# Grouped attention in steps of two batches: one unrolled pipeline over half of the tokens at a time in place of four looped rounds

## The chip, the cores and the metric

The kernel runs on one core of a Trainium2 chip. The metric is the device time of one execution in microseconds, the median of repeated runs. The engines are TensorE (PE; PEld is its weight load), VectorE (DVE), ScalarE (ACT), GpSimd (POOL) and SyncE (SP, which issues the loads).

## The reference

Two layers over 1024 tokens (four batches of 256) of width 256, each an attention and a feed-forward part with a layer norm of the sum behind it. What matters here is the attention inside the last part, with 16 query heads, 4 key and value heads of width 128, rotary embedding and a causal softmax:

```python
H, KV, HD = (16, 4, 128)
def attention(x, wq, wk, wv, wo):
    q = (x @ wq).reshape(b, s, H, HD)
    k = (x @ wk).reshape(b, s, KV, HD)
    v = (x @ wv).reshape(b, s, KV, HD)
    q, k = apply_rope(q, cos, sin), apply_rope(k, cos, sin)
    k, v = jnp.repeat(k, rep, axis=2), jnp.repeat(v, rep, axis=2)
    scores = jnp.einsum('bqhd,bkhd->bhqk', q, k) / np.sqrt(HD)
    scores = jnp.where(causal[None, None], scores, jnp.finfo(scores.dtype).min)
    out = jnp.einsum('bhqk,bkhd->bqhd', jax.nn.softmax(scores, axis=-1), v)
    return out.reshape(b, s, H * HD) @ wo
h = hidden_states + attention(rmsnorm(hidden_states, norm1_w), wq, wk, wv, wo)
```

## The kernel before

The kernel is a chain of blocks, one for each part; in a block every engine has its own program, and the programs meet through semaphores. `layer1_grouped_attention` is the block of this change. It follows a norm that leaves the turned activations as a high and a low part (`c.xTh`, `c.xTl`), and it is followed by the routed experts.

Products of weights and activations are made of three matmuls per 128 rows of contraction (`split_product`: high by low, low by high, high by high), so a projection of 512 tokens to one head is six matmuls of 512 columns. Scores, transposes and values are plain float32.

**Tiling.** A round is one key head with its four query heads, over all 1024 tokens. It has 16 items, an item being one query head in one batch: 256 queries against 256 keys. The causal half is used: 128 queries see 128 keys and the other 128 see 256, so an item has 384 columns of scores. The four rounds are turns of a loop that all engines run (`Fori(0, HKV)`).

**Order.** TensorE's program in a round goes over t from 0 to 19: scores of item t (a mask matmul and two more), at t = 1, 2, 5, 6, 9, 10, 13, 14 half a query projection of the next head (`project_at`), at t = 16 and 17 the two halves of the next round's keys, the output products of item t-4, the three transposes of item t-2, the values of item t-3. Scores and projections take turns on two PSUM banks, 4 and 5, in an order given by `ring`; `freed` makes each wait for whoever last read its bank. Bank 6 has the turned probabilities, bank 7 the values' result, and banks 0 to 3 sum the output projection over all heads of all rounds. Inside a round the items overlap; a round's items are all finished before the next one's scores begin. The last round too projects keys and queries for a round to come.

**The other engines.** VectorE takes the negative maxima of the scores (L1501, L1502), rotates projections (L1478 to L1480: by cosine, then by sine in two halves), takes reciprocals, copies most of the turned probabilities to SBUF (L1518), and makes the low part of an item's result (L1523). It also splits all weights into high and low: the pieces of the next round (L1533, L1535) and each head of wo (L1485, L1487), and copies the round's values out of `v_all` (L1510). ScalarE has the exponentials with their sums (L1555), the high part of the result (L1566), the other turned copies (L1561). GpSimd adds the two products of a rotation (L1452) and multiplies the probabilities by the reciprocals (L1461, L1462). SyncE loads the next round's weights and wo once the last ones are split.

Of the kernel before, what the change touches and what calls it, by code (L numbers as in the profile page):

```python
# [1362 lines left out]
def layer1_grouped_attention(c, pre, spent):  # L1363

    nc, ps = c.nc, c.ps
    PIECES = 1 + GROUP
    with ExitStack() as ctx:  # L1367
        def sb(name, shape, dt=F32):
            return c.tile(ctx, "e_" + name, shape, dt)

        stage, wh, wl, rope = pre.stage, pre.wh, pre.wl, pre.rope
        wo = sb("wo", [P, GROUP, D])
        wo_hi = sb("wo_hi", [P, GROUP, D], F32R)
        wo_lo = sb("wo_lo", [P, GROUP, D], F32R)
        v_all = sb("v_all", [P, NT, HKV * P])
        k_T = spent.stage[:, 0:TOK]
        v = sb("v", [P, NT, P])
        q_T = sb("q_T", [P, 2, TOK])
        by_cos = sb("by_cos", [P, 2, 512])
        by_sin = sb("by_sin", [P, 2, 512])  # L1380
        neg_max = sb("neg_max", [P, 4, 2])
        sums = sb("sums", [P, 4, 2])
        rsum = sb("rsum", [P, 4, 2])
        probs = sb("probs", [P, 4, CAUSAL])
        probsT = sb("probsT", [P, 2, CAUSAL])
        o_hi = sb("o_hi", [P, 2, SEQ], F32R)
        o_lo = sb("o_lo", [P, 2, SEQ], F32R)
        table = sb("table", [P, 1])

        stage_in, wo_in = c.sems(ctx, "e", "stage_in wo_in")  # L1390
        pe_sems = proj_ps, v_ps, s_ps, t_ps, pv_ps, wo_ps = c.sems(ctx, "e", "proj_ps v_ps s_ps t_ps pv_ps wo_ps")
        dve_sems = w_hi, w_split, turned_ps, nm_ready, rs_ready, v_copied, pT_ready, wo_high, wo_split, o_low = c.sems(
            ctx, "e", "w_hi w_split turned_ps nm_ready rs_ready v_copied pT_ready wo_high wo_split o_low")
        act_sems = v_ready, p_ready, o_high = c.sems(ctx, "e", "v_ready p_ready o_high")
        pool_sems = roped, pn_ready = c.sems(ctx, "e", "roped pn_ready")
        block = ctx.enter_context(nc.Block())
        ITEMS = GROUP * BATCH

        ring = []
        for t in range(ITEMS):
            ring.append(("s", t))
            if t % 4 in (1, 2):
                ring.append(("q", 2 * (t // 4 + 1) + t % 4 - 1))
        ring += [("k", 0), ("k", 1)]
        at = {key: n for n, key in enumerate(ring)}
        order = [r for r in ring if r[0] != "s"]
        first = [("k", 1), ("k", 0), ("q", 2 * GROUP), ("q", 2 * GROUP + 1)]  # L1410
        project_at = {t: ("q", 2 * (t // 4 + 1) + t % 4 - 1) for t in range(ITEMS) if t % 4 in (1, 2)}
        project_at |= {ITEMS: ("k", 0), ITEMS + 1: ("k", 1)}

        split_at = {3: 0, 4: 1, 7: 2, 8: 3, 11: 4}

        split_out_at = {5: 3, 9: 0, 12: 1, ITEMS: 2}

        def projected(g, key):
            return LEAD + len(first) + len(order) * g + order.index(key) + 1

        def freed(eng, g, key):

            n = at[key] - 2
            last, g = ring[n % len(ring)], g - 1 if n < 0 else g
            if last[0] == "s":
                eng.wait_ge(p_ready, LEAD + 2 * (ITEMS * g + last[1] + 1))
            else:
                eng.wait_ge(turned_ps, projected(g, last))

        def half_of(key):  # L1430
            return slice(key[1] % 2 * 512, (key[1] % 2 + 1) * 512)
# [12 lines left out]

        @block.gpsimd
        def _(pool):
            give_lead(pool, pool_sems)

            def rotate(key, count, slot):
                pool.wait_ge(turned_ps, count)  # L1450
# [118 lines left out]
        def _(pe):  # L1569
# [17 lines left out]
            for t in range(2):  # L1587
                project_v(t)
# [601 lines left out]
```

## Time and profile before

| | |
|---|---|
| time before, median of 3 runs | 1087.45 us (1087.24 to 1087.92) |
| the profiled execution | 1085.36 us, its span 1083.6 us |
| busy in the span | PE 968.6 (89%), DVE 722.8 (67%), ACT 479.5 (44%), POOL 380.8 (35%) |
| granted TensorE clock, mean over the span | 0.963 |
| the stage from 592.9 to 868.1 us | PE busy 247.4, DVE 211.6, ACT 106.7, POOL 120.0 |

The span is the time from the first instruction to the last; the execution's own time has something around it. Busy shares of an engine are a mean over blocks with different limits, so the stage's own numbers count here. Matmuls overlap in the array, so that TensorE's busy time says less than the distance from one start to the next.

### The profile page before, as it was taken

The page shows a single profiled execution, that of the slowest core. Times are in us where ns is not written, and L with a number is a line of the kernel's source. Part 1 is how long each engine was busy: PE and PEld are TensorE (multiplying, and loading weights), DVE is VectorE, ACT ScalarE, POOL GpSimd, SP SyncE. Part 2 cuts the span into 40 slices and gives each one's busy share as a digit, 9 for nine tenths or more (in the row PEclk, how much of TensorE's full clock was granted, in tenths as well). Part 3 has the DMA queues.
Part 4 walks back from the last instruction along what each step waited for, and adds up shares of the span by engine and source line. Part 5 has one row for each costly group of instructions (what it writes and reads, how often), then busy time and mean ns, then how long its engine had stood idle before and what let it go on. Part 6 is the DMA issues. An engine that isn't in the chain of part 4 may idle for free. (4 is left out here: it accounts for less than half of the span.)

```text
span 1083.6 us, 19692 instructions
## 1 busy us (share of the span) xinstructions
PE 968.6 (89%) x7078; PEld 790.2 (73%) x7087; DVE 722.8 (67%) x1353; ACT 479.5 (44%) x1082; POOL 380.8 (35%) x416
## 2 busy tenths in 40 slices
PE   9788989978999999999997899897989879899970
PEld 5455666647888888788884688786868738899970
DVE  3476767875555555665555687787868767688845
ACT  4221345534445446545444344343434353566630
POOL 2000300005676676576650344453444405000005
PEclk9899989999999999999999999999999979999995
DMA  4000100023324333334321000000104016755503
GB/s 173 1 2 2 30 2 2 2 83 112 109 84 121 110 92 112 105 87 122 108 60 44 5 21 25 19 24 0 44 0 165 0 59 246 279 205 204 205 30 116
DMA packets 55435, 86.87 MB, mean 80 GB/s; under 512 B 4800, under 2 KB 45504, under 8 KB 53184
## 3 DMA queue, kind: packets, MB, share of 16 engines
q1 hardware_dynamic: 53824, 81.66, 23.2%
q0 software_dynamic: 1536, 4.20, 1.2%
q8 instruction: 49, 0.80, 0.3%
q14 instruction: 26, 0.21, 0.1%
HBM read 74.83 MB, written 11.01 MB: 79 GB/s over the span
## 5 line engine op out<-in xcount | busy, mean ns | idle before, releaser
L1555 ACT ACTIVATE e_probs<-ps,e_neg_max 128x128 f32<-128x128 f32 (+1 forms) x128 | 52.8, 417 | 112.7 <-DVE e_neg_max L1502 112.7
L1109 DVE TENSOR_TENSOR d_s_m<-ps,d_decay 128x768 f32<-128x768 f32 x64 | 58.3, 952 | 50.6 <-PE ps L1272 50.6
L123 PE MATMUL ps<-xTl,d_wh 128*128 128x512 f32 x192 | 80.1, 417 | 0.0
L123 PE MATMUL ps<-xTh,d_wh 128*128 128x512 f32 x192 | 76.4, 398 | 0.0
L123 PE MATMUL ps<-xTh,d_wl 128*128 128x512 f32 x192 | 76.3, 397 | 0.0
L123 PE MATMUL ps<-wl_gated,f_wh 128*128 128x256 f32 x240 | 69.1, 288 | 5.8 <-issue 3.7
L1192 ACT ACTIVATE d_gated_hi<-d_gated 128x512 fp32r<-128x512 f32 x32 | 20.2, 632 | 110.6 <-DVE d_gated L1115 110.6
L123 PE MATMUL ps<-wh_gated,f_wl 128*128 128x256 f32 x240 | 68.1, 284 | 0.0
L123 PE MATMUL ps<-wh_gated,f_wh 128*128 128x256 f32 x240 | 68.0, 283 | 0.0
L1452 POOL TENSOR_TENSOR e_q_T<-e_by_cos,e_by_sin 128x512 f32<-128x512 f32 x34 | 43.7, 1287 | 49.4 <-DVE e_by_sin L1480 49.4
L787 ACT ACTIVATE g_probs<-ps,g_neg_max 128x256 f32<-128x256 f32 (+1 forms) x128 | 43.3, 423 | 37.7 <-DVE g_neg_max L730 37.7
L1098 DVE TENSOR_TENSOR wl_gated<-d_q_T,wh_gated 128x512 fp32r<-128x512 f32 x32 | 23.7, 741 | 53.7 <-ACT wh_gated L1171 53.7
L958 POOL TENSOR_TENSOR d_wh<-d_stage,d_nought 128x512 fp32r<-128x512 f32 x32 | 44.3, 1383 | 42.2 <-PE ps L123 29.1
L1821 DVE TENSOR_TENSOR f_wl<-f_stage,f_wh 128x1024 fp32r<-128x1024 f32 x45 | 54.8, 1221 | 5.7 <-ACT f_wh L1947 4.7
L1795 POOL DMA_INDIRECT xT<-slot_outs,f_slots x8 | 7.9, 987 | 143.2 <-DMA slot_outs<-f_rows 141.1
L132 PE MATMUL ps<-warm 128*128 128x512 bf16 x170 | 47.6, 437 | 9.8 <-PEq L1367 3.2
L1461 POOL TENSOR_TENSOR e_probs<-e_probs,e_rsum 128x128 f32<-128x128 f32 x64 | 27.7, 432 | 78.8 <-DVE e_rsum L1507 78.8
L123 PEld LDWEIGHTS ps<-wl_gated,f_wh 128*128 128x128 f32 x240 | 45.6, 190 | 6.4 <-issue 6.3
L123 PE MATMUL ps<-xTl,e_wh 128*128 128x512 f32 x88 | 39.5, 449 | 11.9 <-DVE e_by_sin L1480 5.8
L1947 ACT ACTIVATE f_wh<-f_stage 128x1024 fp32r<-128x1024 f32 x45 | 47.2, 1051 | 6.5 <-DMA f_stage<-in_w_experts 5.1
L966 POOL TENSOR_TENSOR d_wh<-d_stage,d_nought 128x256 fp32r<-128x256 f32 x32 | 26.9, 840 | 63.7 <-PE ps L123 63.7
L123 PEld LDWEIGHTS ps<-xTl,d_wh 128*128 128x128 f32 x192 | 36.5, 190 | 12.8 <-issue 5.5
(364 smaller groups left out, 3203.4 us busy)
## 6 DMA issues: line engine op xcount, KB each, us to landing
f_stage<-in_w_experts SPq DMA_DIRECT2D x15, 1536.0 KB, 6.8
d_decay<-in_decay SPq DMA_DIRECT2D x32, 384.0 KB, 3.8
d_stage<-in_w_decay SPq DMA_DIRECT2D x32, 256.0 KB, 3.4
d_stage<-in_w_decay SPq DMA_DIRECT2D x32, 128.5 KB, 3.5
d_stage_v<-in_w_decay SPq DMA_DIRECT2D x32, 128.0 KB, 2.3
d_stage<-in_w_decay SPq DMA_DIRECT2D x32, 128.0 KB, 2.6
slot_rows<-warm SPq DMA_DIRECT2D x1, 3840.0 KB, 13.6
slot_outs<-f_rows SPq DMA_DIRECT2D x15, 256.0 KB, 2.1
```

Source lines behind the costliest of these rows:

```text
L123: mm = pe.matmul(out, w(k), x(k), start=(n == 0), stop=(n == 3 * len(ks) - 1))
L132: pe.matmul(out, c.warm16[:, 0:P], c.warm16[:, 0:out.shape[1]], start=True, stop=True)
L787: ex = act.activation(probs[:, n % KEPT, i, cols], ps[:, banks(n) + i, cols], ACT.Exp, bias=neg_max[:, n % 4, t, i:i + 1])
L958: pool.tensor_tensor(wh, qk, self.nought[:].unsqueeze(1).broadcast_to((P, KD, 2 * P)), ALU.add).then_inc(self.qk_high, 1)
L966: pool.tensor_tensor(wh, g, self.nought[:].unsqueeze(1).broadcast_to((P, KD, P)), ALU.add).then_inc(self.g_high, 1)
L1098: dve.tensor_tensor(q_lo, q_T[:], q_hi.bitcast(F32), ALU.subtract).then_inc(qk_lo, 1)
L1109: dve.tensor_tensor(s_m[:, s % 2, 2 * b:2 * b + 2, :], ps[:, 2 + 2 * b:4 + 2 * b, 0:CAUSAL], decay[:], ALU.mult).then_inc(sm_ready, 1)
L1452: pool.tensor_tensor(dst, by_cos[:, slot, :], by_sin[:, slot, :], ALU.add).then_inc(roped, 1)
L1461: pool.tensor_tensor(probs[:, u % 4, 0:P], probs[:, u % 4, 0:P], rsum[:, u % 4, 0:1].broadcast_to((P, P)), ALU.mult).then_inc(pn_ready, 1)
L1555: act.activation(probs[:, t % 4, cols], bank[:, cols], ACT.Exp, bias=neg_max[:, t % 4, b:b + 1], accum_out=sums[:, t % 4, b:b + 1]).then_i ...
L1821: dve.tensor_tensor(wl[j % 2][:, cols], stage[j % 2][:, cols], wh[j % 2][:, cols].bitcast(F32), ALU.subtract).then_inc(w_split, 1)
L1947: act.activation(wh[j % 2][:, PARTS[part]], stage[j % 2][:, PARTS[part]], ACT.Copy).then_inc(w_high, 1)
```

## The change

The attention runs unrolled in 32 steps. A step is one query head in two batches: steps 0 to 15 are the 16 heads over the first 512 tokens, steps 16 to 31 the same over the others. Both batches' scores lie in banks 2 and 3, their turned probabilities in 4 and 5, their values' result in 6, every projection in 7, and the output sums of one half in banks 0 and 1, which are read out (`add`) and cleared after the half. VectorE's maxima, copies and reciprocals, ScalarE's and VectorE's parts of the result and GpSimd's multiplications take both batches in one instruction.

In a step TensorE turns the probabilities of step s-2 ahead of the scores of step s, then projects (the queries of step s+2, or first the next keys where s % 4 is 2), then takes the values of step s-2 and the output products of step s-3; in steps with s % 4 = 2 the queries are projected last. Four of the eight value products move from the prologue to the end of steps 8, 9, 11 and 12.

All split weights are kept (`wh_more`, `wl_more`, `wo_hi`, `wo_lo` for all heads), so that the second half splits none. The high parts are now copied by ScalarE, one query head of wo and up to two pieces per step; the low parts of the projections are made by VectorE ahead of the maxima, those of wo by GpSimd. wo comes in 16 loads of one head, four heads ahead. `v_all` is read directly. `by_cos`, `by_sin`, `k_T`, `o_hi`, `o_lo` and `wo` lie in buffers of parts that are done. In `build`, the decay attention's weights are held only until that part is done.

The core of the diff, with eight columns of indentation left out and blank lines omitted:

```diff
+    HALF = TOK // 2
+    STEPS = 2 * HQ
+    PROJ, VALUES_OF = 7, 6
+    KEPT, KEPT_T = 3, 2
...
+def turns_at(s):
+    turns = [("k", (s + 2) // 4)] if s % 4 == 2 and s + 2 < STEPS else []
+    return turns + ([("q", s + 2)] if s + 2 < STEPS else [])
+first = [("k", 0), ("q", 0), ("q", 1)]
+order = first + [key for s in range(STEPS) for key in turns_at(s)]
+nth = {key: n for n, key in enumerate(order)}
+values_at = {8: 4, 9: 5, 11: 6, 12: 7}
+def pieces_at(s):
+    g, j = s // 4 + 1, s % 4
+    return [(g, piece) for piece in ((0, 1), (2, 3), (4,), ())[j]] if g < HKV else []
+pieces = [key for s in range(STEPS) for key in pieces_at(s)]
...
+    for s in range(HQ):
+        if s % 4 == 3 and s // 4 + 2 < HKV:
+            sp.wait_ge(w_split, (1 + GROUP) * (s // 4 + 1))
+            sp.dma_start(stage[:], c.dram["w_grouped"][s // 4 + 2]).then_inc(stage_in, 16)
+        if s + 4 < HQ:
+            sp.wait_ge(wo_split, s + 1)
+            load_out(s + 4)
...
+    def normalised(s):
+        pool.wait_ge(rs_ready, s + 1)
+        for t, cols in enumerate((slice(0, P), slice(P, CAUSAL))):
+            part = probs[:, s % KEPT, :, cols]
+            mul = pool.tensor_tensor(part, part, rsum[:, s % 4, t, :].unsqueeze(2).broadcast_to((P, 2, cols.stop - cols.start)), ALU.mult)
+        mul.then_inc(pn_ready, 1)
+    for key in first:
+        rotate(key)
+    for s in range(STEPS):
+        turns = turns_at(s)
+        for key in turns[:1]:
+            rotate(key)
+        normalised(s)
+        for key in turns[1:]:
+            rotate(key)
+        if s < HQ:
+            pool.wait_ge(wo_high, s + 1)
+            pool.tensor_tensor(wo_lo[:, s, :], wo[:, s % 4, :], wo_hi[:, s, :].bitcast(F32), ALU.subtract).then_inc(wo_split, 1)
...
+    def copy_turned(s):
+        dve.wait_ge(t_ps, s + 1)
+        need(dve, pv_ps, s - KEPT_T + 1)
+        dve.tensor_copy(probsT[:, s % KEPT_T], ps[:, 4:6, 0:CAUSAL]).then_inc(pT_ready, 1)
+    def maxima(s):
+        dve.wait_ge(s_ps, s + 1)
+        need(dve, p_ready, s - 3)
+        pair = ps[:, 2:4, :]
+        dve.tensor_reduce(neg_max[:, s % 4, 0], pair[:, :, 0:P], X, ALU.max, negate=True)
+        dve.tensor_reduce(neg_max[:, s % 4, 1], pair[:, :, P:CAUSAL], X, ALU.max, negate=True).then_inc(nm_ready, 1)
+    def reciprocals(s):
+        dve.wait_ge(p_ready, s + 1)
+        need(dve, pn_ready, s - 3)
+        dve.reciprocal(rsum[:, s % 4], sums[:, s % 4]).then_inc(rs_ready, 1)
+    def low_out(s):
+        dve.wait_ge(o_high, s + 1)
+        dve.tensor_tensor(o_lo[:, s % 2, :], ps[:, VALUES_OF, :], o_hi[:, s % 2, :].bitcast(F32), ALU.subtract).then_inc(o_low, 1)
+    def low_weights(key):
+        g, piece = key
+        dve.wait_ge(w_high, pieces.index(key) + 1)
+        dve.tensor_tensor(wl_more[:, g - 1, piece], stage[:, piece], wh_more[:, g - 1, piece].bitcast(F32), ALU.subtract).then_inc(w_split, 1)
+    def add(half):
+        dve.wait_ge(wo_ps, HQ * (half + 1))
+        for bank in range(2):
+            two = slice(4 * half + 2 * bank, 4 * half + 2 * bank + 2)
+            dve.tensor_tensor(c.y[:, two, :], ps[:, bank, :].rearrange("p (t d) -> p t d", t=2), c.x[:, two, :], ALU.add).then_inc(y_ready, 1)
...
+    for key, bank in zip(first, (PROJ, VALUES_OF, PROJ)):
+        rotate(key, ps[:, bank, :])
+    for s in range(STEPS + 3):
+        if 2 <= s < STEPS + 2:
+            copy_turned(s - 2)
+        if 1 <= s <= STEPS:
+            for key in pieces_at(s - 1):
+                low_weights(key)
+        if s == HQ + 3:
+            add(0)
+        turns = turns_at(s)
+        if s < STEPS:
+            maxima(s)
+        for key in turns[:1]:
+            rotate(key, ps[:, PROJ, :])
+        if s < STEPS:
+            reciprocals(s)
+        if 2 <= s < STEPS + 2:
+            low_out(s - 2)
+        for key in turns[1:]:
+            rotate(key, ps[:, PROJ, :])
+    add(1)
...
+    def exps(s):
+        act.wait_ge(nm_ready, s + 1)
+        need(act, t_ps, s - KEPT + 1)
+        need(act, rs_ready, s - 3)
+        for t, cols in enumerate((slice(0, P), slice(P, CAUSAL))):
+            for i in range(2):
+                ex = act.activation(probs[:, s % KEPT, i, cols], ps[:, 2 + i, cols], ACT.Exp, bias=neg_max[:, s % 4, t, i:i + 1],
+                                    accum_out=sums[:, s % 4, t, i:i + 1])
+        ex.then_inc(p_ready, 1)
...
+    for s in range(STEPS + 2):
+        if s < STEPS:
+            exps(s)
+        if s >= 2:
+            high_out(s - 2)
+        for key in pieces_at(s) if s < STEPS else ():
+            high_weights(key)
+        if s < HQ:
+            high_out_weights(s)
+        if s in values_at:
+            copy_values(values_at[s])
...
-    with pe.Fori(0, HKV) as g:
-        for t in range(ITEMS + 4):
-            if t < ITEMS:
-                b = t % 4
-                if b == 0:
-                    pe.wait_ge(roped, LEAD + len(first) + len(order) * g + 2 * (t // 4))
-                freed(pe, g, ("s", t))
...
+    def free_bank(bank):
+        if bank == PROJ and held:
+            sem, count = held[-1]
+            pe.wait_ge(sem, count)
...
+        g, piece = piece_of(key)
+        if g and key in order[3:]:
+            pe.wait_ge(w_split, pieces.index((g, piece)) + 1)
+        free_bank(bank)
...
+    def scores(s):
+        if s == 0:
+            pe.wait_ge(v_ready, 4)
+        need(pe, p_ready, s)
+        pe.wait_ge(roped, max(nth["q", s], nth["k", s // 4]) + 1)
+        q, keys = q_T[:, s % 2, :], k_T[:, s // 4 % 2, :]
+        for i in range(2):
+            pe.matmul(ps[:, 2 + i, 0:CAUSAL], c.ident16[:], c.neg16[:], start=True, stop=False)
+        for i in range(2):
+            bank, at = ps[:, 2 + i, :], i * SEQ
+            pe.matmul(bank[:, 0:P], q[:, at:at + P], keys[:, at:at + P], start=False, stop=False)
+            mm = pe.matmul(bank[:, P:CAUSAL], q[:, at + P:at + SEQ], keys[:, at:at + SEQ], start=False, stop=True)
+        mm.then_inc(s_ps, 1)
+    def turn(s):
+        pe.wait_ge(pn_ready, s + 1)
+        need(pe, pT_ready, s)
+        if s == 0:
+            pe.wait_ge(v_ready, 4)
+        for i in range(2):
+            for n in range(3):
+                mm = pe.transpose(ps[:, 4 + i, n * P:(n + 1) * P], probs[:, s % KEPT, i, n * P:(n + 1) * P], c.ident)
+        mm.then_inc(t_ps, 1)
...
+        if s == HQ:
+            pe.wait_ge(y_ready, 2)
+            clear()
...
+    for s in range(STEPS + 3):
+        if 2 <= s < STEPS + 2:
+            turn(s - 2)
+        if s < STEPS:
+            scores(s)
+        turns = turns_at(s)
+        for key in turns[:1]:
+            project(key)
+        if 2 <= s < STEPS + 2:
+            values(s - 2)
+        if s >= 3:
+            project_out(s - 3)
+        for key in turns[1:]:
+            project(key)
+        if s in values_at:
+            project_values(values_at[s])
```

## Rows read from the trace of the kernel before

**Rows 1.** The page's first line.
```profile
span 1083.6 us, 19692 instructions
```

**Rows 2.** Windows: prologue and first round; us, engine busy (instructions), PE clock, DMA share, GB/s.
```profile
592.90:613.20 20.30, 19.25 (x75) 14.90 (x76) 11.22 (x18) 5.07 (x9) 5.32 (x4) 0.92 0.16 58
613.20:676.30 63.10, 57.04 (x348) 48.71 (x348) 49.47 (x120) 26.28 (x92) 28.68 (x42) 1.00 0.06 20
```

**Rows 3.** Timeline of TensorE inside round one: start us, us, engine, line, op, form.
```profile
651.52 0.49 PE L1634 MATMUL ps<-consts,e_probs 128*128 128x128 f32 x3
...
654.04 0.49 PE L1634 MATMUL ps<-consts,e_probs 128*128 128x128 f32 x3
654.37 0.60 PE L1643 MATMUL ps<-e_probsT,e_v 128*128 128x256 f32 x2
...
655.02 0.33 PE L1609 MATMUL ps<-neg,ident 128*128 128x384 bf16 x1
...
657.24 0.28 PE L1626 MATMUL ps<-e_wo_lo,e_o_hi 128*128 128x256 f32 x1
...
657.95 0.49 PE L1634 MATMUL ps<-consts,e_probs 128*128 128x128 f32 x3
```

**Rows 4.** Timeline of TensorE: first, sixteenth and next round's first scores.
```profile
613.25 0.33 PE L1609 MATMUL ps<-neg,ident 128*128 128x384 bf16 x1 [0.98 <-ACT e_v_all L1546]
...
662.93 0.33 PE L1609 MATMUL ps<-neg,ident 128*128 128x384 bf16 x1
...
676.39 0.33 PE L1609 MATMUL ps<-neg,ident 128*128 128x384 bf16 x1
```

**Rows 5.** Waits, 613.2 to 868.2: who for whom, us in total, times, longest.
```profile
PEld ps L123 <- DVE e_by_sin L1480: 9.9, 16, 1.8
PEld ps L1609 <- POOL e_q_T L1452: 6.7, 4, 1.7
```

**Rows 6.** Groups by form, 592.9 to 868.2: busy us, mean ns of one, idle before.
```profile
L1452 POOL TENSOR_TENSOR e_q_T<-e_by_cos,e_by_sin 128x512 f32<-128x512 f32 x34 | 43.7, 1287 | 49.4 <-DVE e_by_sin L1480 49.4
L1462 POOL TENSOR_TENSOR e_probs<-e_probs,e_rsum 128x256 f32<-128x256 f32 x64 | 39.2, 613 | 0.0
...
L123 PE MATMUL ps<-xTh,e_wl 128*128 128x512 f32 x88 | 35.4, 402 | 0.0
...
L1478 DVE TENSOR_TENSOR e_by_cos<-ps,e_rope 128x512 f32<-128x512 f32 x44 | 30.0, 681 | 21.6 <-PE ps L123 21.6
...
L1566 ACT ACTIVATE e_o_hi<-ps 128x256 fp32r<-128x256 f32 x64 | 24.6, 385 | 15.4 <-PE ps L1644 14.5
```

**Rows 7.** Timeline of VectorE in the gated attention, where instructions are paired.
```profile
216.32 0.43 DVE L729 TENSOR_REDUCE g_neg_max<-ps 128x2 f32<-128x256 f32 x1 [0.48 <-PE ps L852]
...
217.26 0.95 DVE L735 COPY g_probsT<-ps 128x768 f32<-128x768 f32 x1
```

**Rows 8.** Timeline of ScalarE in round four: an item's exponentials and what follows.
```profile
853.98 0.37 ACT L1555 ACTIVATE e_probs<-ps,e_neg_max 128x128 f32<-128x128 f32 x1 [1.19 <-DVE e_neg_max L1502]
...
854.91 0.39 ACT L1566 ACTIVATE e_o_hi<-ps 128x256 fp32r<-128x256 f32 x1
```

**Rows 9.** Timeline, gated attention: six transposes and the copy that waits for them.
```profile
225.77 0.85 PE L843 MATMUL ps<-consts,g_probs 128*128 128x128 f32 x6 [0.35 <-DVE g_probsT L735]
...
226.66 0.96 DVE L735 COPY g_probsT<-ps 128x768 f32<-128x768 f32 x1 [1.03 <-PE ps L843]
```

**Rows 10.** Timeline: a matmul of the prologue, the additions at the end.
```profile
594.76 0.63 PE L123 MATMUL ps<-xTl,e_wh 128*128 128x512 f32 x1
...
865.56 2.48 DVE L1538 TENSOR_TENSOR y<-ps,x 128x512 f32<-128x512 f32 x4 [0.61 <-PE ps L1626]
```

**Rows 11.** Tile e_wo: splits on VectorE; ns min/median/max, first and last start.
```profile
L1485 DVE CAST e_wo_hi<-e_wo x19: 279/1147/1179, 608.9 to 858.8; 128x256 fp32r<-128x256 f32 x19
L1487 DVE TENSOR_TENSOR e_wo_lo<-e_wo,e_wo_hi x19: 424/425/1402, 609.3 to 860.0; 128x256 fp32r<-128x256 f32 x19
```

**Rows 12.** DMA issues: one grouped weight load, KB, median us to landing.
```profile
e_stage<-in_w_grouped SPq DMA_DIRECT2D x5, 640.0 KB, 4.0
```

More of the change, by code:

```diff
@@ L1407, in layer1_grouped_attention @@
[L1407 to L1431, printed above, removed]
+        stage, rope = pre.stage, pre.rope
+        wh_more = sb("wh_more", [P, HKV - 1, 1 + GROUP, KD, P], F32R)
@@ L1482, in _ @@
-            dve.wait_ge(pre.tables_in, 16)
-            def split_out(head, n):
-                dve.tensor_copy(wo_hi[:, head], wo[:, head]).then_inc(wo_high, 1)
-                dve.wait_ge(wo_high, LEAD + n)
-                dve.tensor_tensor(wo_lo[:, head], wo[:, head], wo_hi[:, head].bitcast(F32), ALU.subtract).then_inc(wo_split, 1)
-            for n, key in enumerate(first):
-                rotate(key, LEAD + n + 1, n % 2, ps[:, 4 + at[key] % 2, :])
-            dve.wait_ge(wo_in, 16)
-            for head in range(GROUP - 1):
-                split_out(head, head + 1)
@@ L1586, in _ @@
-            project(first[1])
-            for t in range(2):
-                project_v(t)
-            for bank in range(4):
-                pe.matmul(ps[:, bank, :], c.warm16[:, 0:P], c.warm16[:], start=True, stop=False, skip_group_check=True)
-            pe.wait_ge(turned_ps, LEAD + 2)
-            project(first[2])
-            for t in range(2, 4):
-                project_v(t)
-            pe.wait_ge(turned_ps, LEAD + 3)
-            project(first[3])
-            for t in range(4, NT):
-                project_v(t)
@@ new lines, in project_values, with clear @@
+                if bank == PROJ:
+                    held.append((v_ready, t + 1))
+            def clear():
+                for bank in range(2):
+                    pe.matmul(ps[:, bank, :], c.warm16[:, 0:P], c.warm16[:], start=True, stop=False, skip_group_check=True)
+            def scores(s):
[11 more added lines that the diff above has]
+                mm.then_inc(s_ps, 1)
@@ new lines, in project_out @@
+            def project_out(s):
+                head = s % HQ
+                if s < HQ:
+                    pe.wait_ge(wo_split, head + 1)
+                if s == HQ:
+                    pe.wait_ge(y_ready, 2)
+                    clear()
+                for o, ws, ready in ((o_hi, (wo_lo, wo_hi), o_high), (o_lo, (wo_hi,), o_low)):
+                    pe.wait_ge(ready, s + 1)
+                    for t in range(4):
+                        for w in ws:
+                            mm = pe.matmul(ps[:, t // 2, t % 2 * D:(t % 2 + 1) * D], o[:, s % 2, t * P:(t + 1) * P], w[:, head, :],
+                                           start=False, stop=False, skip_group_check=True)
+                mm.then_inc(wo_ps, 1)
```

285 lines of the change are left out of this document (99 added, 186 removed).

## The prediction

> **What bounds the kernel now.** I read the page first: the span is 1083.6 us [rows 1]. Then I cut the trace into stretches. The grouped attention runs from 592.9 to 868.2, one prologue of 20.3 us and four identical rounds of 63.1 us, TensorE busy in 57 of the 63.1 and at clock 1.00, VectorE busy in 49.5, the others under 29 [rows 2]. Nothing outside this stage is changed, so the sum is made inside it.
>
> TensorE's timeline inside a round gives the price of its work. Two items without a projection start 2.52 us apart (651.52 to 654.04), one with a projection takes 3.91 (654.04 to 657.95), so a projection costs 1.39 us and an item 2.52: transposes 0.33, values 0.65, scores some 0.83, output products 0.71 [rows 3]. The work of the whole stage is thus 64 items, 161.3 us, plus projections. There are 4 before the loop and 10 in each of four rounds, and 8 value products of the same six matmuls: 52 x 1.39 = 72.3. The four clearing matmuls are under 1, I take 0.8. Together 234.4 us out of 275.4 (592.9 to 868.3). TensorE stands still, or waits, for 41.0 us.
>
> Where these 41 us lie is seen from the first instruction of each item (L1609). The first scores of round one stand at 613.25 and the sixteenth at 662.93, the next round begins at 676.39 [rows 4]. From the sixteenth scores to the next round the work is 4 transposes less one already done, 4 value and 5 output products and 2 projections, about 0.8 + 1.0 + 2.6 + 3.5 + 2.8 = 10.7, but it takes 13.46. The first four items of a round lack most of their older work, yet the round as a whole is 63.1 against 16 x 2.52 + 13.9 = 54.2. So a round loses 8.9 us, four lose 35.6, mostly because each fills and drains the pipeline of items. The waits agree: TensorE's loads wait for the rotation on VectorE 9.9 us and the scores for the rotated queries on GpSimd 6.7 [rows 5], both at such places. TensorE's order of work is the bound, with bubbles at the loop's ends.
>
> **The change, part by part.** *Fewer projections.* The loop's last round projects keys and queries for a fifth group that doesn't exist, 4 x 1.39 = 5.6 us. The new order has 8 key and 32 query projections: 40, and 8 value products. Work: 161.3 + 48 x 1.39 + 0.8 = 228.8.
>
> *One pipeline of 32 steps instead of four of 16 items.* Per step TensorE does turn(s-2), scores(s), a projection, values(s-2), out(s-3): 1.39 + 2 x 2.52 = 6.43 us. Whether the others keep up I work out with prices of paired instructions. VectorE: a rotation is 3 instructions of about 0.69 at 0.70 spacing, 2.12; low_out of 512 columns is priced as one of them, the same kind of instruction of the same width from the same memories [rows 6]. The gated attention has the pair forms already: both maxima issue in 0.94 us and end within 1.02, the 768-wide copy takes 0.95 [rows 7]. With a reciprocal of 0.15 a plain step asks 0.95 + 1.02 + 2.12 + 0.17 + 0.72 = 5.0 us of VectorE. ScalarE: the four exponentials with read-outs of one item end 0.93 after they begin (853.98 to 854.91) [rows 8], so 1.86 a step, plus high_out at no more than twice today's 0.385 for half its width, 0.77, and up to three weight copies of 0.385: under 3.8. GpSimd: 1.29 for a rotation, 0.61 and 1.29 for the two normalisations [rows 6], and 0.65 for wo_lo: 3.9. A step with a key projection (s = 2, 6, ..., 26) adds 2.12 to VectorE and 1.39 to TensorE. So TensorE is the longest in each.
>
> Being longest is not enough where engines wait in order, so I followed a plain step from the moment turn(s-2) begins. From TensorE's slot to VectorE's start I count 0.24, from six transposes of 0.65 at 225.77 to the copy at 226.66 [rows 9]; back and to ScalarE 0.1. TensorE: turn to 0.65, scores to 2.3, projection to 3.7, values to 5.0, out to 6.4. VectorE: copy 0.9 to 1.85, maxima 2.5 to 3.55, rotation 3.9 to 6.0, reciprocal 6.2, low_out 6.3 to 7.0. ScalarE: exponentials 3.6 to 5.5, high_out to 6.2. Then each wait of TensorE is met ahead of time: values want the copy (1.85 against 3.7), the next scores the exponentials, since banks 2 and 3 are now single (5.5 against 7.1), the next projection its bank (6.0 against 8.7), the next out low_out (7.0 against 11.4), turn(s) the normalised probabilities (about 8.1 against 12.9). The move of the transposes ahead of the scores costs nothing: their data are a whole step old, and the scores behind them have 1.6 us of room. What is late next is the rotation after a key step: two rotations run to 2.4 into the next step, where TensorE wants the bank at 2.3, a wait of about 0.2, 7 times (the first of them counted with the start, below).
>
> *The waits that stay*, followed the same way. Slow clock at the head as now: some seven matmuls of 0.63 instead of 0.40 [rows 6, 10], at 0.2 each 1.4 us. Before the first scores 0.6 (they wait for value copy 4, whose bank they use). Steps 0 to 3 lack old work and run on the chain scores, maxima, exponentials and normalisation: 23.5 us for 18.9 of work, 4.6. Key steps 1.3. Step 11, where a key's late rotation meets a value product in the same bank, 0.5. Step 19, where add(0) of 1.4 us stands ahead of the maxima, 0.8. Steps 30 on, 23.6 us for 18.1 of work, with the last two additions (now four, 2.48 us [rows 10]) in it, 5.5, and 0.3 to the next block. Sum 15.0. Stage: 228.8 + 15.0 = 243.8, or 31.6 less than 275.4.
>
> *Weights split once.* The high halves move to ScalarE, where some 2.5 us of each step are free; the output weights' low halves move to GpSimd. VectorE keeps 15 subtractions in 9 steps (s = 1, 2, 3 mod 4, up to 11), ahead of the maxima. Alone one takes 0.424. But this very form has once taken 1.402, and the cast ahead of it, 0.279 at best, has a median of 1.147 [rows 11]: GpSimd was at work beside it. So a collision is worth 0.87 to 0.98. GpSimd normalises just then (0.9 to 2.8 of a step), so I expect most of the 15 to meet it. Bounds: none exposed, 0 (a gain is excluded, the subtractions are done today as well); all 15 at 0.98 exposed, 14.7. The scores' 1.6 us of room takes most of it; I put in 2.0. The Trainium skill, "SBUF — State Buffer", in the part on the memory's doors, says of this pair of engines that the one that starts first holds the shared port for its whole instruction; the spread of 279 to 1179 ns for one form agrees with that, and by its rule every one of the 15 would wait out the rest of a 0.6 or 1.3 us instruction, which is the upper bound's case.
>
> *Loads.* SyncE issues 16 smaller loads of wo in place of 5, each four steps ahead of use, and three of the stage, each issued a step before ScalarE wants it; 640 KB land in 4.0 us [rows 12], a step is 6.4. The later ones are issued only after w_split, so step 4's copy comes nearest, with 2 us of room, and ScalarE is not the bound there. The copy of v (four of them) and the table loads in the loop go; they lie on VectorE and ScalarE and I cost them at nothing. Below nothing they can't go: TensorE's stream is counted whole.
>
> **The sum.** -31.6 + 2.0 = -29.6 us. The profiled execution took 1085.4 us for its span of 1083.6; the median of the runs is 1087.45, 2.1 more than it. The difference is carried over: a span of about 1054 and a median of 1087.45 - 29.6 = 1057.9, about 1058.
>
> **The rivals.**
> *A, forecast*: TensorE's order sets the pace, small waits. 1053 to 1063.
> *B, fewer waits*: the first steps fill faster than I think and no split is exposed. The 15.0 falls to 10, nothing for collisions: 1087.45 - 36.6 = 1051. For it: the middle of today's rounds goes at 2.52 and 3.91 without a stop [rows 3]. Against it: the fill hangs on the chain of one item, which is priced from rows.
> *C, VectorE binds in the splitting steps*: three rounds with 5 subtractions each, VectorE 4 x 5.0 + 2.12 + 5 x 1.41 = 29.2 us against TensorE's 27.1 in a round, and all collisions exposed: 1056 + 14.7 = 1071, half exposed 1064. For it [rows 11]; against it, GpSimd is idle half the time.
> *D, the other side, TensorE's clock*. In the prologue now, after TensorE stood still ahead of this block, matmuls ran at 0.63 instead of 0.40 and the stretch shows 0.92 granted, that is partly the lower level, 1.2 of 2.4 GHz [rows 2, 6, 10]. If the new order's short stops (bank 7 freed late, single score banks) let the clock fall again and again, work done at the lower level costs its time once more. It decides from 29.6 us of full-speed work on, an eighth of the 228.8; at a sixth, 38 us, the result is 1096. Against it: the loop of today has longer stops at each round's end and shows 1.00. The Trainium skill, "TensorE: Matmul & The Clock Gate", under the second failure mode, warns that going round PSUM banks with small stops makes the clock swing; today's rounds don't bear it out.
> That the change doesn't do what it says isn't a case here: the four wasted projections and three of the drains are gone by the order of instructions alone.
>
> **How the numbers follow.** Chances: A 0.60, B 0.13, C 0.23, D 0.04. The time is A's, 1058. The range takes B to its 1051 and 2 more for a bound of my fill, and C up to its 1071: 1049 to 1071, leaving out D and the ends of B and C. A measurement of this kernel tells about 0.2%, 2.2 us, from no change. Faster holds A, B, C: 0.96; within 0.2% 0.01; slower 0.03.
>
> **What would show it.** In the changed kernel: about 244 to 246 us from the first projection to the last addition; steps 6.4 us apart by their first mask matmul, 7.8 to 8.0 where a key or value product joins; clock 1.00 after the prologue; TensorE's longest waits only in steps 0 to 3 and from 30 on; the maxima pair at 1.02, the copy at 0.95. The subtraction of wl_more with a mean over 1.0 us would speak for C; steps 4 to 11 well above 6.5 too. I am wrong if plain steps late in the stage (20 to 29) are above 6.8 us: then a loop through VectorE that I held to be met binds, or the clock does.

## The result, and the profile after

The changed kernel takes 1050.58 us in the median of 4 runs (1049.55 to 1051.54), against 1087.35 for four runs of the kernel before: a ratio of 0.9666, 95% interval 0.9648 to 0.9683, so 36.8 us less. The forecast was 1058, in a range of 1049 to 1071: the direction and the range hold, and the time is 7.4 us better than forecast, which is rival B's 1051.

The profiled execution took 1049.55 us. The page of the changed kernel, its first line and busy times, against [rows 1]:

```profile
span 1047.7 us, 18378 instructions
...
PE 948.7 (91%) x7053; PEld 785.2 (75%) x7063; DVE 693.9 (66%) x1150; ACT 459.8 (44%) x1038; POOL 375.9 (36%) x364
```

The changed kernel cut into the prologue up to the first scores, and the rest of the stage (columns as in [rows 2]):

```profile
590.30:601.50 11.20, 10.84 (x48) 8.55 (x50) 6.20 (x9) 3.12 (x5) 3.86 (x3) 1.00 0.33 105
601.50:830.90 229.40, 220.98 (x1396) 196.22 (x1395) 175.64 (x290) 83.78 (x324) 110.79 (x117) 1.00 0.10 31
```

TensorE is busy in 221 of 229.4 us at clock 1.00; VectorE, the next, in 176. In [rows 2] a round had 57 of 63.1. The clock of the prologue is 1.00 where it was 0.92.

The timeline of the changed kernel: the start of the stage, the first scores and five late ones (L1626 is the first matmul of a step's scores, L123 a projection), and the last addition:

```profile
590.35 0.47 PE L123 MATMUL ps<-xTl,e_wh 128*128 128x512 f32 x1 [1.14 <-PEq L491]
590.65 0.40 PE L123 MATMUL ps<-xTh,e_wl 128*128 128x512 f32 x1
...
600.81 0.50 PE L1626 MATMUL ps<-neg,ident 128*128 128x384 bf16 x2 [0.24 <-ACT e_v_all L1546]
...
768.55 0.49 PE L1626 MATMUL ps<-neg,ident 128*128 128x384 bf16 x2
...
774.96 0.49 PE L1626 MATMUL ps<-neg,ident 128*128 128x384 bf16 x2
...
781.36 0.49 PE L1626 MATMUL ps<-neg,ident 128*128 128x384 bf16 x2
...
789.17 0.49 PE L1626 MATMUL ps<-neg,ident 128*128 128x384 bf16 x2
...
795.80 0.49 PE L1626 MATMUL ps<-neg,ident 128*128 128x384 bf16 x2
...
829.55 1.29 DVE L1516 TENSOR_TENSOR y<-ps,x 128x512 f32<-128x512 f32 x2 [1.52 <-PE ps L1668]
```

Plain steps are 6.41 us (768.55, 774.96, 781.36). The step with a key projection takes 7.81 and the one behind it 6.63, which is 0.22 more than a plain step. From the first projection (590.35) to the end of the last addition (829.55 + 1.29 = 830.84) the **stage** takes 240.49 us. The same two marks before are 592.95 and 868.04: 275.09. The stage gave 34.6 us. Two further profiles of this kernel gave 240.49 and 240.50, while the medians of its total time lay up to 2 us apart between series and single executions reached from 1049.4 to 1056.0. So the experiments are read by the stage where they are small.

The waits of the changed kernel from 590 to 833 (who for whom, us in total, times, longest):

```profile
ACT e_probs L1554 <- DVE e_neg_max L1496: 129.0, 32, 7.5
...
PEld ps L1653 <- DVE e_probsT L1489: 3.2, 3, 1.6
...
PEld ps L1626 <- ACT e_probs L1554: 3.1, 2, 1.9
...
PE ps L123 <- DVE xT L1484: 1.2, 1, 1.2
...
PEld ps L123 <- DVE xT L1484: 0.6, 2, 0.3
```

ScalarE's idle time is 129 us; it isn't the bound. TensorE's own waits for other engines stand in one to three places each. In [rows 5] its weight loads waited 9.9 us for the rotation on VectorE, in 16 places; now it is 0.6 in two (and 1.2 before one matmul), and the 6.7 us for the rotated queries on GpSimd have gone. The longest waits lie in steps 0 to 2 and from step 30 on, as the prediction had it.

Groups by form of the changed kernel, 591 to 845 (columns as in [rows 6]). The parts of an item's result now lie in the buffers `wh_gated` and `wl_gated`, so L1561 is `high_out` and L1505 `low_out`:

```profile
L1459 POOL TENSOR_TENSOR e_probs<-e_probs,e_rsum 128x512 f32<-128x512 f32 x32 | 33.9, 1060 | 0.0
...
L1489 DVE COPY e_probsT<-ps 128x768 f32<-128x768 f32 x32 | 30.6, 955 | 14.0 <-PE ps L1640 13.8
...
L1496 DVE TENSOR_REDUCE e_neg_max<-ps 128x2 f32<-128x512 f32 x32 | 21.7, 679 | 0.0
...
L1505 DVE TENSOR_TENSOR wl_gated<-ps,wh_gated 128x512 fp32r<-128x512 f32 x32 | 21.6, 674 | 5.9 <-ACT wh_gated L1561 5.2
...
L1561 ACT ACTIVATE wh_gated<-ps 128x512 fp32r<-128x512 f32 x32 | 19.3, 602 | 7.4 <-PE ps L1654 7.4
```

The tile of the low weight parts in the changed kernel (ns min/median/max, first and last start), the subtraction that rival C rested on:

```profile
L1510 DVE TENSOR_TENSOR e_wl_more<-e_stage,e_wh_more x15: 415/746/1506, 606.3 to 679.2; 128x256 fp32r<-128x256 f32 x15
```

One of them in step 7, with what stood beside it on GpSimd:

```profile
648.28 0.96 DVE L1489 COPY e_probsT<-ps 128x768 f32<-128x768 f32 x1
649.16 0.75 DVE L1510 TENSOR_TENSOR e_wl_more<-e_stage,e_wh_more 128x256 fp32r<-128x256 f32 x1
...
648.33 1.29 POOL L1453 TENSOR_TENSOR e_q_T<-xT 128x512 f32<-128x512 f32 x1 [1.04 <-DVE xT L1484]
...
650.87 0.37 ACT L1554 ACTIVATE e_probs<-ps,e_neg_max 128x128 f32<-128x128 f32 x1 [5.67 <-DVE e_neg_max L1496]
```

The subtraction ends at 649.91, 0.29 after GpSimd's addition (649.62). Eleven of the 15 stand beside GpSimd, take 0.46 to 1.51 us, and each ends 0.27 to 0.29 after a GpSimd instruction has ended. The four others, which start at most 0.09 us before the end of GpSimd's work, take 0.415 to 0.419.

### The profile page after: what moved, and what is told of

It reads as the page before. It is cut to its first block and busy times, and to the rows that moved or that the text cites. A ratio compares the mean times of both kernels' runs of the same rounds, so it can differ in the third digit from the quotient of the medians.

```text
span 1047.7 us, 18378 instructions
## 1 busy us (share of the span) xinstructions
PE 948.7 (91%) x7053; PEld 785.2 (75%) x7063; DVE 693.9 (66%) x1150; ACT 459.8 (44%) x1038; POOL 375.9 (36%) x364
## 5 line engine op out<-in xcount | busy, mean ns | idle before, releaser
L1554 ACT ACTIVATE e_probs<-ps,e_neg_max 128x256 f32<-128x256 f32 (+1 forms) x128 | 52.2, 420 | 129.0 <-DVE e_neg_max L1496 129.0
L123 PE MATMUL ps<-xTl,d_wh 128*128 128x512 f32 x192 | 80.0, 416 | 0.0
L123 PE MATMUL ps<-xTh,d_wh 128*128 128x512 f32 x192 | 76.2, 397 | 0.0
L123 PE MATMUL ps<-xTh,d_wl 128*128 128x512 f32 x192 | 76.1, 396 | 0.0
L123 PE MATMUL ps<-wl_gated,f_wh 128*128 128x256 f32 x240 | 70.4, 293 | 6.2 <-issue 4.1
L1453 POOL TENSOR_TENSOR e_q_T<-xT 128x512 f32<-128x512 f32 x32 | 41.0, 1283 | 83.1 <-DVE xT L1484 83.1
L123 PE MATMUL ps<-wh_gated,f_wl 128*128 128x256 f32 x240 | 69.3, 289 | 0.0
L123 PE MATMUL ps<-wh_gated,f_wh 128*128 128x256 f32 x240 | 69.0, 288 | 0.0
L1459 POOL TENSOR_TENSOR e_probs<-e_probs,e_rsum 128x256 f32<-128x256 f32 x64 | 52.6, 844 | 6.5 <-DVE e_rsum L1501 6.5
L123 PEld LDWEIGHTS ps<-wl_gated,f_wh 128*128 128x128 f32 x240 | 46.9, 196 | 6.8 <-issue 6.7
L132 PE MATMUL ps<-warm 128*128 128x512 bf16 x170 | 43.4, 407 | 8.4 <-PEq L1018 3.1
L1998 ACT ACTIVATE f_wh<-f_stage 128x1024 fp32r<-128x1024 f32 x45 | 47.2, 1051 | 6.9 <-DMA f_stage<-in_w_experts 5.5
L123 PEld LDWEIGHTS ps<-wh_gated,f_wl 128*128 128x128 f32 x240 | 47.0, 196 | 0.0
L123 PEld LDWEIGHTS ps<-wh_gated,f_wh 128*128 128x128 f32 x240 | 47.0, 196 | 0.0
```

Source lines behind the costliest of these rows:

```text
L123: mm = pe.matmul(out, w(k), x(k), start=(n == 0), stop=(n == 3 * len(ks) - 1))
L132: pe.matmul(out, c.warm16[:, 0:P], c.warm16[:, 0:out.shape[1]], start=True, stop=True)
L1453: pool.tensor_tensor(dst, by_cos[:, n % 2, :], by_sin[:, n % 2, :], ALU.add).then_inc(roped, 1)
L1459: mul = pool.tensor_tensor(part, part, rsum[:, s % 4, t, :].unsqueeze(2).broadcast_to((P, 2, cols.stop - cols.start)), ALU.mult)
L1554: ex = act.activation(probs[:, s % KEPT, i, cols], ps[:, 2 + i, cols], ACT.Exp, bias=neg_max[:, s % 4, t, i:i + 1], accum_out=sums[:, s % ...
L1998: act.activation(wh[j % 2][:, PARTS[part]], stage[j % 2][:, PARTS[part]], ACT.Copy).then_inc(w_high, 1)
```

## The experiments

Ten start from the changed kernel, two from the kernel before. Each total has its ratio to the kernel before, run beside it on the same chip.

**The changed kernel again**, at both ends of the work, as the measure of repetition.

> The changed kernel as it stands, once more beside the kernels of this series. Every theory: 1050.6 us, within 1, ratio to before 0.9666.

> The changed kernel once more, beside the kernels of this series: ratio to before 0.967 to 0.970.

1050.23 us (0.9698, 0.9674 to 0.9722) and 1052.09 (0.9667, 0.9648 to 0.9687). Stages 240.49 and 240.50.

**Turning behind the scores**, the old order inside a step:

```diff
-    if 2 <= s < STEPS + 2:
-        turn(s - 2)
     if s < STEPS:
         scores(s)
+    if 2 <= s < STEPS + 2:
+        turn(s - 2)
```

> The changed kernel with one swap in TensorE's order: scores of step s first, then the transposes of step s-2. Same work. My working of a step puts it so: the copy of the turned probabilities then starts 2.7 us into the step instead of 0.9, the maxima end at 4.7, the exponentials at 6.6, and the next scores, now at the head of the step at 6.4, wait 0.3 us in a plain step and 1.4 us in the nine steps where weight subtractions stand between copy and maxima; 0.5 after each key step. Sum 12 to 24 us slower than the changed kernel, about 1068. Rival: the transposes' data are a step old and their place doesn't matter: 0 to 3 us slower.

1064.55 us (0.9806, 0.9785 to 0.9827); stage 250.80, 10.3 more, a little under the band of 12 to 24 and far above the 0 to 3 of the rival. Its timeline: the scores of step 6, then those of step 7 and what follows them:

```profile
644.29 0.50 PE L1626 MATMUL ps<-neg,ident 128*128 128x384 bf16 x2 [0.36 <-ACT e_probs L1554]
...
653.26 0.50 PE L1626 MATMUL ps<-neg,ident 128*128 128x384 bf16 x2
...
655.76 0.96 DVE L1489 COPY e_probsT<-ps 128x768 f32<-128x768 f32 x1 [0.21 <-PE ps L1640]
...
656.64 0.57 DVE L1510 TENSOR_TENSOR e_wl_more<-e_stage,e_wh_more 128x256 fp32r<-128x256 f32 x1
...
657.47 0.68 DVE L1496 TENSOR_REDUCE e_neg_max<-ps 128x2 f32<-128x512 f32 x1
...
658.18 0.37 ACT L1554 ACTIVATE e_probs<-ps,e_neg_max 128x128 f32<-128x128 f32 x1 [5.67 <-DVE e_neg_max L1496]
...
659.95 0.50 PE L1626 MATMUL ps<-neg,ident 128*128 128x384 bf16 x2
```

VectorE does the copy ahead of the maxima. With the turning behind the scores the copy of step 7 starts 2.50 us after the step's scores, and the exponentials, which free the single score banks, begin 4.92 after them. In the changed kernel it is 1.67 and 4.26 (scores at 646.61, shown below). The delay costs nothing where there is room for it: plain steps stay at 6.42, and step 7 itself at 6.69. It is paid in step 2 (1.8), in steps 3, 5, 6, 9 and 10 (0.5 to 0.9 each), in steps 8 and 12 and the later key steps (0.1 to 0.2 each), in step 19 (0.3), and in steps 30 and 31 with what follows them (2.9), where the values wait 1.05 to 1.10 for the copy. So the move of the turning ahead of the scores is worth 10.3 us.

**Four drains**: the new steps, but every 8 steps all finish before the next begin.

```diff
+def steps():
+    for start in range(0, STEPS, 8):
+        for i in range(11):
+            yield start + i, i < 8, 2 <= i < 10, i >= 3
-for s in range(STEPS + 3):
+for s, new, old, out in steps():
```

> The changed kernel with its 32 steps cut into four rounds of 8: each round is finished (turn, values, output products of its last steps) before the scores of the next begin, on all engines. Same instructions. Theory that the change's gain is mostly the filling and draining of the pipeline: each of the three restarts costs what the trace of the changed kernel shows for its one filling (24.9 us for 18.9 of work in steps 0 to 3) and its one draining (2 to 3 us without the additions), 8 us, so 24 us slower (18 to 30), about 1075. Rival, the gain is in paired instructions and unrolling: under 8 us slower.

1074.68 us (0.9912, 0.9884 to 0.994); stage 262.61, 22.1 more, where 24 was expected. TensorE's timeline at the first restart:

```profile
655.36 0.82 PE L1645 MATMUL ps<-consts,e_probs 128*128 128x128 f32 x6
...
657.47 0.70 PE L1658 MATMUL ps<-e_probsT,e_v_all 128*128 128x256 f32 x2 [1.30 <-DVE e_probsT L1494]
...
662.19 0.70 PE L1658 MATMUL ps<-e_probsT,e_v_all 128*128 128x256 f32 x2 [1.05 <-DVE e_probsT L1494]
...
666.45 0.50 PE L1631 MATMUL ps<-neg,ident 128*128 128x384 bf16 x2
...
671.83 0.50 PE L123 MATMUL ps<-e_wvl,xTh 128*128 128x512 f32 x1 [2.19 <-DVE xT L1489]
...
673.34 0.50 PE L1631 MATMUL ps<-neg,ident 128*128 128x384 bf16 x2
```

Each restart has a few stops of 1 to 2.2 us, for the copy of a step that has nothing beside it, then for the rotation. From the last scores of each eight to the next scores it is 17.09, 16.77 and 16.83 us, in place of 6.6. In this order of steps one pipeline in place of four is worth 22.1 us.

**Parts of the change in the kernel before**: first the loop unrolled alone, then also without the fifth group's projections.

```diff
-with pe.Fori(0, HKV) as g:
+for g in range(HKV):
```

```diff
+def asked(g, t):
+    return t in project_at and (g < HKV - 1 or t < 4 * (GROUP - 1))
```

> The kernel before with its four rounds written out on every engine instead of looped, all instructions and their order kept. Theory that the loss lies in filling and draining: 0 to 3 us faster than before (the loops' heads alone), about 1086. Rival, the loop itself is what costs: 8 us faster or more.

> The same written-out kernel without the four projections (queries and keys) that the last round makes for a fifth group, and without their rotations. Theory: 4 projections of 1.39 us leave TensorE's path, 5.6 us faster than the written-out one, up to 1 more where one of them waited for its bank. Rival, they lie in stops that the last round has anyway: under 2 us.

1083.67 us (0.9956, 0.9938 to 0.9975) and 1079.38 (0.9926, 0.9897 to 0.9955). The two marks of each stage, of the unrolled kernel:

```profile
594.09 0.47 PE L123 MATMUL ps<-xTl,e_wh 128*128 128x512 f32 x1 [2.04 <-PEq L491]
...
866.62 0.68 DVE L1538 TENSOR_TENSOR y<-ps,x 128x512 f32<-128x512 f32 x1
```

and of the one without the fifth group:

```profile
594.01 0.47 PE L123 MATMUL ps<-xTl,e_wh 128*128 128x512 f32 x1 [2.04 <-PEq L491]
...
862.51 0.68 DVE L1541 TENSOR_TENSOR y<-ps,x 128x512 f32<-128x512 f32 x1
```

273.2 and 269.2: 1.9 us for the unrolling, 4.0 for the projections where their work is 5.6, a little under the 5.6 expected. The rest of that work probably filled bubbles of the last drain; no run shows it by itself. Both kernels keep the stop of 2.04 us ahead of the stage.

**Two suspected costs doubled** on VectorE: the low weight parts, and one of the maxima.

```diff
+dve.tensor_tensor(wl_more[:, g - 1, piece], stage[:, piece], ..., ALU.subtract).then_inc(once, 1)
+dve.wait_ge(once, pieces.index(key) + 1)
 dve.tensor_tensor(wl_more[:, g - 1, piece], stage[:, piece], ..., ALU.subtract).then_inc(w_split, 1)
```

```diff
+dve.tensor_reduce(again[:, s], pair[:, :, P:CAUSAL], X, ALU.max, negate=True)
 dve.tensor_reduce(neg_max[:, s % 4, 0], pair[:, :, 0:P], X, ALU.max, negate=True)
```

> The changed kernel with each of the 15 subtractions of wl_more made twice, the second after the first. VectorE gets 15 x 0.76 = 11.5 us more work ahead of the maxima in nine steps. Theory (TensorE's order is the bound and the scores have 1.6 us of room): in steps with one piece nothing, in the six with two pieces some of the room is overrun, 0 to 5 us slower than the changed kernel. Rival C of the prediction (VectorE binds in the splitting steps): 9 to 12 us slower.

> The changed kernel with one more 512-column maximum (0.68 us, its result unused) ahead of the two real ones in each of the 32 steps, 21.8 us more of VectorE, on the way from scores to exponentials. Theory: a plain step asks 5.7 us of VectorE against TensorE's 6.4 and the way has 1.6 us of room, so 0 to 5 us slower than the changed kernel, all of it in steps 0 to 2, after key steps and in the last two. Rival, VectorE is near the bound: 15 us slower or more.

Subtractions twice: 1060.89 us (0.9754, 0.973 to 0.9778), stage 248.59, 8.1 more, between the two expectations and outside both. A maximum twice in all 32 steps: 1060.14 (0.9751, 0.9726 to 0.9775), stage 245.76, 5.3 more, just over the 0 to 5 and far from the rival's 15. Scores of steps 5, 6 and 7 with the subtractions twice:

```profile
639.09 0.49 PE L1629 MATMUL ps<-neg,ident 128*128 128x384 bf16 x2
...
645.61 0.50 PE L1629 MATMUL ps<-neg,ident 128*128 128x384 bf16 x2
...
655.72 0.49 PE L1629 MATMUL ps<-neg,ident 128*128 128x384 bf16 x2
```

and in the changed kernel:

```profile
638.49 0.49 PE L1626 MATMUL ps<-neg,ident 128*128 128x384 bf16 x2
...
646.61 0.49 PE L1626 MATMUL ps<-neg,ident 128*128 128x384 bf16 x2
...
653.24 0.49 PE L1626 MATMUL ps<-neg,ident 128*128 128x384 bf16 x2
```

Step 5 is 6.52 against 6.41; step 6, with a key and two pieces, is 10.11 against 8.12. The added subtractions, two to a step, cost 2.0 to 2.1 in each of steps 1, 2 and 6, but only 0.1 in steps 5 and 9 and 0.4 in step 10; the one of step 11 costs 0.9. The added maximum costs 0.6 in step 0, 1.45 in step 2, 1.25 in step 6, 0.6 in step 11, 0.1 to 0.2 in steps 1, 5 and 19, and 0.95 in steps 30 and 31 with what follows them. In 22 of the 32 steps this instruction of 0.68 us, on the way from the scores to the exponentials, changes nothing, step 10 with its key and two pieces among them. So VectorE has room in most steps and none in the filling steps, in steps 6 and 11, and at the end.

**The mask matmuls left out**, so that scores are not masked and the output is that of another attention:

```diff
-for i in range(2):
-    pe.matmul(ps[:, 2 + i, 0:CAUSAL], c.ident16[:], c.neg16[:], start=True, stop=False)
...
```

> The changed kernel without the two mask matmuls of each step, so the scores are not causal. TensorE has 0.325 us less in each of 32 steps, the others the same. Theory (TensorE's order is the bound): 9 to 10.4 us faster, the plain step 6.09 instead of 6.41. Rival, VectorE or the way through the exponentials binds: under 4 us.

1043.56 us (0.9594, 0.9573 to 0.9615); stage 233.86, 6.6 less, between the 9 to 10.4 of the theory and the under 4 of the rival. Plain steps fall by 0.33 to 6.08, but the steps behind a key step keep their 6.63, steps 1, 2 and 11 keep their length too, and step 6 grows by 0.32. There TensorE doesn't set the time. The wait that grew in this kernel, from one place to ten, is the projection's for the bank that the rotation of the keys frees:

```profile
PE ps L123 <- DVE xT L1484: 4.4, 10, 1.4
```

**Value products elsewhere**: at the ends of steps 0, 1, 8 and 9, the first two of them in bank 6; then also the pieces of weights spread, so that one step of four has two pieces and the others one (steps 2, 6 and 10 have one).

```diff
-values_at = {8: 4, 9: 5, 11: 6, 12: 7}
+values_at = {0: 4, 1: 5, 8: 6, 9: 7}
...
```

```diff
-for piece in ((0, 1), (2, 3), (4,), ())[j]
+for piece in ((0, 1), (2,), (3,), (4,))[j]
```

> The changed kernel with value products 4 and 5 moved from steps 8 and 9 to the ends of the projections' part of steps 0 and 1, into bank 6, which is free until the first values, and 6 and 7 done in steps 8 and 9. TensorE stands 1.65 us in step 0 and 2.1 in step 1, each more than a product's 1.39, and step 11 loses its stop of 0.6. Theory: 2.2 to 3.8 us faster than the changed kernel, about 1047.4. Rival: the first steps are bound by a chain that the extra copies on ScalarE lengthen: 0 to 1 us faster.

> The kernel with value products 4 and 5 in steps 0 and 1, and with the weight pieces spread, so that no key step has two subtractions on VectorE (two, one, one, one per group instead of two, two, one, none). Theory: the stage is 3.1 us shorter for the products, as it was in their own trace, and up to 0.5 for step 6's stop of 0.3: 236.9 to 237.4 us against 240.5, the whole 3.3 us faster than the changed kernel. Rival: spreading makes the load of the next group late, and step 5 or 9 waits: back to 238 or more.

Stages 237.38 (3.1 less: step 11 falls from 8.43 to 6.65, step 12 from 7.80 to 6.40, for work that now fills holes of the first two steps) and 236.80. The scores of steps 6 and 7 there:

```profile
641.41 0.49 PE L1633 MATMUL ps<-neg,ident 128*128 128x384 bf16 x2
...
649.22 0.49 PE L1633 MATMUL ps<-neg,ident 128*128 128x384 bf16 x2
```

Step 6 falls from 8.12 to 7.81 and step 2 from 7.78 to 7.59: with one piece in them they have little or no stop. The totals, 1050.86 (0.9687, 0.9673 to 0.97) and 1049.58 (0.9662, 0.9635 to 0.9688), can't be told from the changed kernel's. Both gains are shown in the stage alone.

**Semaphore increments at the head of TensorE's program**, as the kernel before had there for its loop:

```diff
+give_lead(pe, [c.norm_sems[-1]] * 6)
```

> The changed kernel with six semaphore increments at the head of TensorE's program, as give_lead makes in the kernel before; nobody waits for them. Theory: they are what kept TensorE still for 2.04 us instead of 1.14 ahead of the first projection, and the clock falls after the longer stop: first projection 0.9 us later, some seven matmuls at 0.63 instead of 0.39, so 2.3 us slower. Rival: the increments are free or the clock doesn't fall, under 1 us.

1056.19 us (0.9712, 0.9691 to 0.9733); stage 242.15. TensorE's timeline in it:

```profile
593.79 0.47 PE L123 MATMUL ps<-xTl,e_wh 128*128 128x512 f32 x1 [2.05 <-PEq L491]
...
594.83 0.63 PE L123 MATMUL ps<-xTh,e_wl 128*128 128x512 f32 x1
```

The stop ahead of the stage is 2.05 us as in the kernel before (1.14 after), and matmuls go at 0.63 a little later, as in [rows 10]; the granted clock of the prologue is 0.86 instead of 1.00. Together 0.9 and 1.7 us, 2.6 for six increments, with 2.3 expected. The total is 4.1 us above the changed kernel's of the same series; the 1.5 beyond the 2.6 are within what profiles of the same kernel differ by outside the stage.

## Why the prediction was right, and where its size was off

**What bounded the kernel** was read rightly: TensorE's order, with bubbles where each round filled and drained. The stage's 34.6 us come apart into 1.9 (unrolling), 4.0 (fifth group), 22.1 (one pipeline in place of four) and the difference of 6.6 between the last kernel of the parts (269.19) and the new steps with four drains (262.61). About 1.7 of the 6.6 is the slow clock at the head, which the run with the increments prices; the other 4.9 is the paired work and its order, which no run took apart. The parts hold for this order of steps between the two kernels: the 22.1 was measured with the new steps, and no run took the drains out of the old loop of single items.

**The plain step**, 6.43, measured 6.41, and with a key 7.8, measured 7.79 plus 0.22 behind it (0.2 forecast). The pair forms held: both maxima 1.02 from start to end (1.02), copy 0.955 (0.95), normalisations 1.06 and 0.627 (1.29 and 0.61), low_out 0.674 (0.69), high_out 0.602 (0.77 at most). The wide normalisation had been priced by the rotation's 1.29 in [rows 6], which was too high, but off the path.

**Where 7.4 us too much came from.** The two profiled executions differ by 35.8 us, against a forecast of 29.6. In four stretches of the stage, by the first matmul of steps:

| | forecast | measured |
|---|---|---|
| first projection to first scores | 12.35 | 10.46 |
| steps 0 to 3 | 24.15 | 24.87 |
| steps 4 to 29 | 186.1 | 182.95 |
| from the scores of step 30 | 22.95 | 22.21 |
| together | 245.5 | 240.49 |

The forecast column is the prediction's sum at the marks of the trace. Its steps began with the transposes, 0.65 us ahead of the scores, which moves 23.5 to 24.15 and 23.6 to 22.95. Steps 4 to 29 are 26 x 6.43, 10 extra products of 1.39, 0.4 of clearing, 2.6 of waits and the 2.0 for collisions; the first row is what remains.

The first term that was mis-sized is *"Slow clock at the head as now"*, 1.4 us. It measured nothing in the changed kernel. I held it for a property of the block's place; it hung on the six instructions of TensorE's entry, which the change removes with the loop. The experiment with the lead brings back both the longer stop and the 0.63, and prices the slow matmuls at 1.7. The 0.9 of the stop, outside the stage, was not in my sum at all.

The second is the 2.0 for collisions. The subtractions were lengthened (mean 764 ns against 415 to 419 alone, 5.2 us for all 15), but most of it lies inside the room. What shows is 0.3 in step 6 and 0.2 in step 2, which go when those steps have one piece in place of two. The rest of the difference in steps 4 to 29 is the plain step, 0.02 under its forecast 26 times (0.5), and some 0.9 of small terms that came out below their forecast. The single stops of my list held: step 11 0.63 (0.5), step 19 0.65 (0.8), behind key steps 0.22 (0.2). At the head 0.5, and at the end 0.7, weren't taken apart. The first steps went the other way, 0.7 longer than forecast.

That makes 5.0 in the stage. Of the 35.8 between the profiled executions, 34.6 is the stage, 0.9 the stop, and 0.3 the balance of parts whose code is the same: those ahead of the stage were some 1.7 shorter, those behind it some 1.3 longer, and three profiles of the changed kernel alone differ there by 2.6 and 2.4. The last 1.0, up to the 36.8 of the medians, is of that kind too. So about 5.9 of the 7.4 has a place; the rest is scatter, and that the total meets rival B's 1051 so closely is in part luck.

**"The move costs nothing"** was right and said too little. The room of 1.6 us behind the scores is itself a product of the turning ahead of them; without it the stage is 10.3 us longer.

**The rivals.** B, fewer waits, has the time right, 1051, and the reason by half: splits are exposed by some 0.5 only, but the first steps didn't fill faster (24.87 against 24.15); the head did. C asked for subtractions over 1.0 us and steps well above 6.5 in 4 to 11: the mean is 0.764, and the steps without key or values in that stretch are 6.40 to 6.63. The doubled subtractions say how near it was: twice the work there costs 8.1 us. C's price was too high because it took the longest case, 0.98 more, for every subtraction; the lengthening depends on how much of GpSimd's instruction is left, and its mean was 0.35. The Trainium skill, "SBUF — State Buffer", "Who interferes with whom", says that a VectorE instruction with two inputs in SBUF contends with a GpSimd instruction that reads SBUF, and that the one that issues first keeps the shared port for its whole instruction. The trace agrees: eleven of 15 subtractions end 0.27 to 0.29 us after the end of a GpSimd instruction, and the four that start with at most 0.09 us of it left take 0.415 to 0.419. D is refuted for this order: clock 1.00 through 229 us, with stops of up to 1.5 us before matmuls. The Trainium skill, "TensorE: Matmul & The Clock Gate", "A second HAM failure mode: psum-queue depth-cycling", tells of a bf16 kernel that went round PSUM banks with small stops and whose clock swung between its levels; the changed kernel doesn't show it either.

**What stays open.** The 4.9 us of paired work and its order are known only as a remainder. The theory that TensorE's order is the whole bound is too simple: without 0.33 us of work per step, 32 steps give back 6.6 and not 10.4. Behind key steps, in steps 6 and 11 and in the filling steps something else sets the distance; the waits there are for VectorE's rotations and for the exponentials. Why two added subtractions cost 2.0 us in step 6 but only 0.4 in step 10, which has a key as well, wasn't taken apart; steps 8 and 9, whose value products give TensorE 1.4 us more each and VectorE none, may let VectorE catch up ahead of step 10.

## What to carry to other kernels

Count how often a pipeline fills and drains before counting instructions: here three restarts were worth 22.1 us, the useless projections 4.0 of their 5.6, and the loop's own overhead 1.9. Before an order is changed, write down the room of each single buffer in a step (ready time against wanted time); what lies inside it is free, and the same 0.68 us that is free in 22 of 32 steps costs 1.25 to 1.45 in steps 6 and 2, where a key's rotation and two pieces of weights already meet. Look for what an edit removes at a block's head: a few semaphore instructions there can cost a stop and, behind it, a fall of the clock.

## What the runs showed of the hardware that I had not expected

Six semaphore instructions at the head of TensorE's program made the stop ahead of the block 2.05 us instead of 1.14. Some 1 to 1.5 us into the block that follows the longer one, matmuls of 512 columns go at 0.63 us for a while (granted clock 0.86 over the 12 us of the prologue, so partly the lower of the two levels); after the shorter one they stay at 0.39 to 0.40 (clock 1.00).

A VectorE subtraction of 128x256 takes 415 to 419 ns alone and 462 to 1506 with GpSimd at work beside it, and then it ends 0.27 to 0.29 us after GpSimd's instruction does. The lengthening, 5.2 us in all, cost TensorE some 0.5 that the runs show; two more such instructions in a step cost up to 2.1 us.
